# A four-layer attention and adapter kernel: the first tile's weight folding and tables in a new order, the narrow weight products with exchanged sides, and filled waits at the end

## The chip, the cores and the metric

The kernel runs on one core of a Trainium2 chip. It is one program with an instruction stream for each engine: TensorE (PE; its weight loads are shown as PEld), VectorE (DVE), ScalarE (ACT), GpSimd (POOL) and SyncE (SP), which only issues DMAs. The streams are written by hand and meet at semaphores. The metric is the device time of one execution in microseconds.

## The reference

The input x is 32 sequences of 64 tokens with 512 features, in float32. Four residual layers follow one another.

```
x = x + attention(x)          # 8 query heads, 4 key heads of 64; rms norm, rotation;
                              # the new keys and values go into a paged cache of 16-token
                              # blocks, and 256 positions of it are attended to
x = x + W1[subject] applied to each sequence           # 64 x 64 matrix per sequence
x = x + x@W_base.T + scale*(((x@Wt.T)@A[e].T)@B[e].T)@Wp.T   # e: adapter of the sequence
x = x + x@W.T + scale3*((x@A3[e3].T)@B3[e3].T)
```

## The kernel before

**Tiles.** The 2048 tokens are 16 tiles of 128 (two sequences each). A prologue makes the new keys and values of all tiles (`key_tile`, 16 of them), stores them to `newkv` in DRAM (`store_kv`, L364), and prepares the weights. Then one loop body is run per tile: attention of tile t, and, interleaved with it on every engine, the layers after attention of tile t-1. The last tile's rest has no attention beside it and stands alone at the end (`end = Tile(4, 0)`).

**Folding.** Layers 3 and 4 are both linear, so the kernel works with the product of their weights. `m23` is (W_base + I)(W + I), 512 x 512, made in four pieces by `fold(k)` (L1145, four matmuls each of 128 x 512 in float32); ScalarE and VectorE split each piece into a high and a low part (`m23_high` L677, `m23_low` L960). The identity is added to both weights by `add_identity` on GpSimd (L499) after their loads (SyncE, L394, from step `LATE_A` of the loop on). The adapters are folded as well: `down2` is Wt times A and `up2t` is Wp times B, each made by `narrow` (L1261: for each of four blocks of 128 rows four matmuls, the weight as the stationary side, 64 columns moving); `down3` is W_base's block times A3 (L1261, 128 columns moving), `cross` and `up2` are products of `up2t` with A3 and W (L1145), and four tables `up_s` are made by `carried(e)` on TensorE (L1299) and `carry(e)` on VectorE (L1116). SyncE stores the tables to DRAM, and for each tile the sequences' rows are picked from them.

**Names in the loop body on TensorE.** `queries` (L1152, L1157: query product of the next tile, in high and low parts), `queries_t` (L1204: its transposes), `keys_t` (L1308: transposes of gathered keys), `scores` (L1322), `probs_t` (L1335: transposes of probabilities), `values` (L1346: two heads in two halves of the array's columns), `project` (L1152, L1157), `layer1` (L1369), `ranks` (L1380), `layer3` (L1390), `layer3_low` (L1395), `layer3_ranks` (L1400). Scalar copies of `layer1`'s result are L744 and L739, the residual is L1049, the output copy is L754.

**GpSimd's order.** It computes inverse roots for the key tiles (`root`, L481), then adds the identities, then gathers cache rows (L512, L519) and the new keys (`lay_over`, L526) for the first attention batches, which waits for all stores of `newkv`.

**The eight PSUM banks** are `gb`, `sbk`, `tb`, `ob`, two of each. In the first tile `fold(2)` and `fold(3)` use `ob`, and `carried` uses `gb` and `ob`. Parts of the SBUF are used first for setup and later for the loop: the new order needs `wb_s`, `w3_s` and the tables for longer.

## Time and profile before

| | |
|---|---|
| median of 3 runs | 456.7 us (456.54 to 456.89) |
| profiled execution | 458.0 us, its span 456.2 us |
| mean granted TensorE clock | 0.985 of full |
| PE busy | 440.8 us (97%) |
| DVE, ACT, POOL busy | 308.8, 262.0, 228.5 us |
| DMA queues moved | 67.40 MB, mean 148 GB/s |

The span runs from the first to the last instruction; the execution's own time is 1.8 us longer. Three parts of the span matter below: the key tiles to about 63.5 us, the preparation and the first tile to about 129 us, and the end from about 441 us; between the last two lie fifteen loop bodies. In a list in order of time a line gives start, duration, engine, code line and operation, with the idle time before it and who ended it in brackets. The count of matmul rows is twice the number of float32 matmuls.

### The profile page before, as it was taken

What the parts mean: (1) busy time and instruction counts of PE and PEld (TensorE: products, weight loads), DVE (VectorE), ACT (ScalarE), POOL (GpSimd) and SP (SyncE); (2) the same over time, 40 slices, a digit from 0 to 9 for tenths busy, and PEclk for the clock granted to TensorE, in tenths of its full rate; (3) what the DMA queues carried; (4) which work ended last, traced back from release to release, by engine and by line L of the source; (5) the groups of instructions that cost most, each with busy time, mean ns of one, the idle gap of its engine ahead of it and who ended that gap; (6) DMA issues with size and microseconds to landing.
All of it is one profiled execution on the core that took longest, in us unless ns stands there. A gap on an engine that the chain in (4) does not pass through costs nothing.

```text
span 456.2 us, 10436 instructions
## 1 busy us (share of the span) xinstructions
PE 440.8 (97%) x3039; PEld 316.7 (69%) x3039; DVE 308.8 (68%) x899; ACT 262.0 (57%) x772; POOL 228.5 (50%) x245
## 2 busy tenths in 40 slices
PE   8999996999699999999999999999999999999996
PEld 3444884466377778777877777777777787777764
DVE  4688878655667677776767676767777676757531
ACT  0756850354357575756666475757575666656641
POOL 0225469665655657374655655564747465341000
PEclk9999997999899999999999999999999999999998
DMA  6577796264826465565647373746456563533131
GB/s 211 192 246 250 214 349 200 85 175 109 272 62 185 93 170 130 143 163 112 178 91 209 62 214 65 198 102 166 134 137 145 138 197 72 158 61 66 28 70 53
DMA packets 75593, 67.40 MB, mean 148 GB/s; under 512 B 50869, under 2 KB 51253, under 8 KB 75538
## 3 DMA queue, kind: packets, MB, share of 16 engines
q1 hardware_dynamic: 60208, 37.97, 30.9%
q0 software_dynamic: 14400, 28.05, 22.6%
q10 hardware_dynamic: 930, 0.72, 0.6%
q8 instruction: 25, 0.41, 0.4%
q14 instruction: 30, 0.25, 0.2%
HBM read 72.49 MB, written 10.22 MB: 181 GB/s over the span
## 4 chain that ended last, share of the span: by engine, by line
PE 90%; DVE 3%; issue 2%; POOL 2%; DMA 1%; ACT 1%; DVEq 0%; POOLq 0%; ACTq 0%
PE gb L1152 13%; PE sbk L1322 10%; PE ob L1346 10%; PE tb L1335 9%; PE gb L1181 7%; PE gb L1390 7%; PE gb L1157 6%; PE tb L1308 5%; PE gb L1395 4%; PE gb L1369 3%; PE gb L1400 3%; PE ob L1145 2%; PE ob L1380 2%; PE gb L1204 2%; PE sbk L1209 1%
## 5 line engine op out<-in xcount | busy, mean ns | idle before, releaser
L1031 DVE CUSTOM_DVE_ANT_0 wide<-sbk,mask 128x336 f32<-128x336 f32 x128 | 60.0, 505 | 63.4 <-PE sbk L1322 63.1
L728 ACT ACTIVATE pt_s<-tb 112x384 f32<-112x384 f32 x128 | 55.6, 488 | 53.5 <-PE tb L1335 53.5
L722 ACT ACTIVATE wide<-wide,negmax 128x336 f32<-128x336 f32 x128 | 72.6, 571 | 22.0 <-DVE negmax L1031 21.2
L526 POOL DMA_INDIRECT windows_more<-newkv,idx_b x48 | 49.0, 1021 | 61.9 <-issue 50.1
L526 POOL DMA_INDIRECT windows<-newkv,idx_b x48 | 49.8, 1038 | 47.7 <-issue 40.4
L1335 PEld LDWEIGHTS tb<-cst_late,wide 128*112 128x112 f32 x384 | 44.4, 133 | 18.9 <-issue 11.1
L1335 PE MATMUL tb<-cst_late,wide 128*112 128x128 f32 x384 | 52.5, 273 | 2.3 <-DVE wide L1044 1.5
L1322 PE MATMUL sbk<-kt_s,qt_s 64*128 64x336 f32 x256 | 52.8, 489 | 0.0
L1044 DVE TENSOR_SCALAR wide<-wide,rinv 128x336 f32<-128x336 f32 x128 | 45.4, 397 | 2.3
L716 ACT ACTIVATE kt_s<-tb 128x336 f32<-128x336 f32 x64 | 25.4, 449 | 13.3 <-PE tb L1308 13.2
L1181 PE MATMUL gb<-wkv_s,xt_s 128*128 128x512 f32 x72 | 31.9, 596 | 0.0
L481 POOL TENSOR_TENSOR k_rstd<-k_ms,half 128x4 f32<-128x4 f32 x16 | 18.9, 1181 | 23.1 <-DVE k_ms L892 23.0
L481 POOL TENSOR_TENSOR q_rstd<-q_ms,half 128x8 f32<-128x8 f32 x16 | 26.8, 1676 | 6.2 <-DVE q_ms L892 5.8
L890 DVE TENSOR_REDUCE q_ss<-q_sq 128x8 f32<-128x512 f32 x16 | 11.0, 686 | 25.8 <-ACT q_sq L652 25.8
L652 ACT ACTIVATE q_sq<-gb 128x512 f32<-128x512 f32 x15 | 9.0, 597 | 32.5 <-PE gb L1157 32.5
L1390 PE MATMUL gb<-m_hi,x_hi 128*128 128x512 f32 x64 | 27.3, 427 | 0.0
L1152 PE MATMUL gb<-wo_hi,ot_hi 128*128 128x512 f32 x64 | 26.5, 414 | 0.6 <-ACT ot_hi L734 0.6
L1390 PE MATMUL gb<-m_lo,x_hi 128*128 128x512 f32 x64 | 25.9, 404 | 0.0
L1346 PEld LDWEIGHTS ob<-pt_s,windows 112*64 112x64 f32 x384 | 20.6, 137 | 7.4 <-issue 3.7
L1346 PEld LDWEIGHTS ob<-pt_s,windows_more 112*64 112x64 f32 x384 | 20.6, 137 | 7.2 <-issue 3.9
L1322 PEld LDWEIGHTS sbk<-kt_s,qt_s 64*128 64x128 f32 x256 | 19.4, 185 | 8.9 <-issue 8.7
L1152 PE MATMUL gb<-wo_lo,ot_hi 128*128 128x512 f32 x64 | 25.2, 393 | 0.0
(217 smaller groups left out, 1026.8 us busy)
## 6 DMA issues: line engine op xcount, KB each, us to landing
xt_s<-xt_dram SPq DMA_DIRECT2D x31, 256.0 KB, 4.7
newkv<-kvo SPq DMA_DIRECT2D x16, 256.0 KB, 3.6
xtok_s<-xtok_dram SPq DMA_DIRECT2D x16, 256.0 KB
up_sel<-up_tab SPq DMA_DIRECT2D x128, 32.0 KB
out_dram<-xo SPq DMA_DIRECT2D x16, 256.0 KB, 4.1
down_sel<-down_tab SPq DMA_DIRECT2D x64, 32.0 KB
wkv_s<-wkv_dram SPq DMA_DIRECT2D x4, 256.0 KB, 6.1
wide<-wt_dram SPq DMA_DIRECT2D x4, 256.0 KB, 5.3
```

What stands on the lines that cost most here:

```text
L481: nc.gpsimd.tensor_tensor(nr[w]["rstd"][:], nr[w]["ms"][:], half[:, 0:h], ALU.pow).then_inc(S[w + "_rstd"], 1)
L526: nc.gpsimd.indirect_dma_start(kv_s[r][:, c, :], None, newkv, bass.IndirectOffsetOnAxis(ap=idx_b[r][:, (1, 2, 4)[c]:(1, 2, 4)[c] + 1], axi ...
L722: nc.scalar.activation(prob[i][:, g, :], neg_s[:, g, :], ACT.Exp, bias=negmax[:, g:g + 1], scale=-1.0, accum_out=psum_p[i][:, g:g + 1]).th ...
L728: nc.scalar.activation(pt_s[g][:], tb[g % 2][0:KP, 0:CH * 128].rearrange("p (c q) -> p c q", c=CH), ACT.Copy).then_inc(S["pt_ev"], 1)
L1031: V.tensor_tensor_reduce(out=neg_s[:, g, :], in0=sbk[g % 2][:, 0:WK], in1=mask[(t.part(u) + k) % 2][:], scale=-1.0 / 16, scalar=3.0e38, op ...
L1044: V.tensor_scalar(prob[i][:, g, :], prob[i][:, g, :], rinv[i][:, g:g + 1], None, ALU.mult).then_inc(S["prob_ready"], 1)
L1152: last = mm(bank, lhs(0, c), rhs(b, c), start=(c == 0 and b == 0), stop=False)
L1181: last = mm(gb[n % 2][:], xt_s[r][:, c, :], wkv_s[:, c, :], start=(c == 0), stop=(c == C - 1))
L1322: mm(sbk[h][:, 0:WK], qt_s[half_rows, 256 * p + 128 * v:256 * p + 128 * v + 128], kt_s[p][half_rows, :], start=True, stop=True).then_inc(S ...
L1335: last = nc.tensor.transpose(tb[g % 2][0:KP, 128 * c:128 * c + 128], prob[i][:, g, KP * c:KP * c + KP], ident)
L1346: last = mm(ob[u][64 * h:64 * h + 64, 128 * p:128 * p + 128], kv_s[r][:, c, 256 + 64 * g:320 + 64 * g], pt_s[g][:, c, :], start=(c == 0), ...
L1390: mm(gb[0][:], x2s[0][:, c, :], m23_s[b][:, c, :], start=(c == 0 and b == 0), stop=False)
```

## The change

It reorders preparation and the first loop body on every engine, and edits the end.

- `narrow` for `down2` and `up2t` is replaced: the 64-column adapter matrix is the stationary side, the weight's 512 columns move, `down2` in the lower 64 output rows and `up2t` in the upper 64 of one bank, alternately, eight matmuls in all. One copy (`both_s`), four transposes and two copies bring the result into the old layout.
- The identities are added by VectorE after key tiles 13 and 14; the weights' loads begin two steps earlier in SyncE's loop (`LATE_A` 8 for 10).
- In the first tile's body, `queries_t(2)` waits for three pieces' low parts (`m23_lo` 3) and the last `values` for four. ScalarE's `m23_high(2)` stands behind its `probs_t(0, 3)` there, `m23_high(3)` behind `probs_t(1, 1)`.
- `fold(0)` and `fold(1)` stay ahead of the first tile, `fold(2)` and `fold(3)` move into it; the four `carried` and `carry` move from the first tile to before it (`carry` on VectorE within its first norms), with other banks. `queries_t(1)` moves behind `down3` and `cross`, the first scores behind `up2`.
- On VectorE the first `query_tile` comes after the low parts; on GpSimd the first `lay_over` comes before the second gathers.
- At the end, one of the two copies of `layer1`'s result goes to VectorE, and two extra matmuls of 384 columns whose result nobody reads (`stay_awake`) stand behind `project` and behind `layer1`.
- The SBUF tensors of the loop are allocated in another order, with gaps; SyncE and ScalarE get waits that protect the shared regions.

```diff
@@ shared
-        LATE_A = TILES // 2 + 2
+        LATE_A = TILES // 2
@@ SyncE, tile
+                if first:
+                    sp.wait_ge(S["m23_mm"], C)
                 after(sp, S["x1_ready"], t.n(1, 0))
                 sp.dma_start(xtok_s[:], xtok[t.n(1, 0)]).then_inc(S["l_xtok"], 16)
@@ GpSimd
             root("k", 4, 16)
-            add_identity(wb_s, ("l_wb", 16 * C), "wb_ident")
-            add_identity(w3_s, ("l_w3", 16 * C), "w3_ident")
-            gather_pair(t0, 0, 1)
-            gather_single(t0, 0, 1)
...
             lay_over(t0, 0, 0)
+            gather_pair(t0, 0, 1)
+            gather_single(t0, 0, 1)
             root("q", 8, 1)
+            pool.wait_ge(S["l_scl"], 48)
+            pool.wait_ge(S["l_ab3"], 32)
+            P.tensor_scalar(b3_s[:], b3_s[:], scl3[:], 1.0, ALU.mult, ALU.mult).then_inc(S["b3_scaled"], 1)
             lay_over(t0, 0, 1)
-            pool.wait_ge(S["up2t_mm"], 1)
+            pool.wait_ge(S["both_mm"], 1)
@@ ScalarE, ahead of the loop
+            evac(both_s, ob[0][:], "both_mm", "both_ev")
+            both = ob[1][:].rearrange("p (c w r) -> p w c r", c=C, w=2)
+            evac(down2_s[:].rearrange("p e c r -> p c e r"), both[:, 0].rearrange("p c (e r) -> p c e r", e=NE2), "both_t_mm", "down2_ev")
+            evac(up2t_s[:], both[:, 1].unsqueeze(2).to_broadcast([128, C, 2, 64]), "both_t_mm", "up2t_ev")
             m23_high(0, tb[0])
             split_high(5)
-            square(1, sbk[0])
+            m23_high(1, tb[1])
             split_high(6)
             split_high(7)
-            m23_high(1, tb[1])
-            queries(1, 0, sbk[1])
-            m23_high(2, ob[0])
+            square(1, sbk[0])
             xq_high(2, xt_s[0], 32)
-            m23_high(3, ob[1])
@@ ScalarE, behind keys(Tile(0, 0), 0, 0)
-            exps(Tile(0, 0), 0, 0, 0)
-            exps(Tile(0, 0), 0, 0, 1)
             evac(down3_s[:].rearrange("p e c r -> p c e r"),
                  gb[0][:].rearrange("p (c e r) -> p c e r", c=C, e=NE3), "down3_mm", "down3_ev")
-            exps(Tile(0, 0), 0, 0, 2)
-            exps(Tile(0, 0), 0, 0, 3)
             evac(cross[:], ob[1][:, 0:64], "cross_mm", "cross_ev")
+            queries(1, 0, sbk[1])
+            act.wait_ge(S["up2_mm"], 1)
+            act.wait_ge(S["l_scl"], 48)
+            nc.scalar.activation(up2_s[:], gb[1][:], ACT.Copy, scale=scl2[:]).then_inc(S["up2_ev"], 1)
+            for g in range(G):
+                exps(Tile(0, 0), 0, 0, g)
@@ ScalarE, end
-            layer1(end)
+            act.wait_ge(S["l1_mm"], TILES)
+            nc.scalar.activation(x2t[:, :, 0:64], gb[1][:, 0:256].rearrange("p (c t) -> p c t", c=C), ACT.Copy).then_inc(S["x2_ready"], 1)
+            act.wait_ge(S["x2_half"], 1)
@@ VectorE
                 key_tile(n)
+                if n == 13:
+                    add_identity(wb_s, "l_wb", "wb_ident")
+                elif n == 14:
+                    add_identity(w3_s, "l_w3", "w3_ident")
...
+            m23_low(0, tb[0])
             split_low(4)
-            m23_low(0, tb[0])
-            dve.wait_ge(S["qtab_ready"], 1)
-            query_tile(Tile(0, 0), 0, None, None, None, sbk[0])
             split_low(5)
             m23_low(1, tb[1])
             split_low(6)
             split_low(7)
+            dve.wait_ge(S["qtab_ready"], 1)
+            query_tile(Tile(0, 0), 0, None, None, None, sbk[0])
@@ VectorE, tile
                 norm(t, 0, 0, (0, 1))
                 if first:
-                    dve.wait_ge(S["cross_ev"], 1)
-                    V.tensor_tensor(cross_s[:], cross[:].unsqueeze(1).to_broadcast([128, NE3, 64]),
-                                    con("hot3").unsqueeze(2).to_broadcast([128, NE3, 64]), ALU.mult).then_inc(S["cross_ready"], 1)
+                    for e in range(NE3 // 2):
+                        carry(e)
...
                 def between():
                     if first:
-                        carry(0)
-                        carry(1)
+                        m23_low(2, gb[1])
...
                 if first:
-                    carry(2)
-                    carry(3)
+                    m23_low(3, ob[1])
@@ VectorE, end
             attn_residual(end)
+            dve.wait_ge(S["l1_mm"], TILES)
+            V.tensor_copy(x2t[:, :, 64:128], ob[1][:, 0:256].rearrange("p (c t) -> p c t", c=C)).then_inc(S["x2_half"], 1)
@@ TensorE, ahead of the loop
-            narrow(ob[0], 64, lambda c, k: wt_s[:, c, 128 * k:128 * k + 128], lambda c: a2_s[:, c, :]).then_inc(S["down2_mm"], 1)
             pe.wait_ge(S["l_wpt"], 16 * (C + 1))
-            narrow(ob[1], 64, lambda c, k: wpt_s[:, c, 128 * k:128 * k + 128], lambda c: b2_s[:, c, :]).then_inc(S["up2t_mm"], 1)
+            for c in range(C):
+                mm(ob[0][0:64], a2_s[:, c, :], wt_s[:, c, :], start=(c == 0), stop=(c == C - 1))
+                last = mm(ob[0][64:128], b2_s[:, c, :], wpt_s[:, c, :], start=(c == 0), stop=(c == C - 1))
+            last.then_inc(S["both_mm"], 1)
             pe.wait_ge(S["wb_ident"], 1)
             pe.wait_ge(S["w3_ident"], 1)
             pe.wait_ge(S["idx_ready"], 1)
-            fold(0)
+            fold(0, tb[0])
+            pe.wait_ge(S["both_ev"], 1)
+            for c in range(C):
+                last = nc.tensor.transpose(ob[1][:, 128 * c:128 * c + 128], both_s[:, 128 * c:128 * c + 128], ident)
+            last.then_inc(S["both_t_mm"], 1)
+            fold(1, tb[1])
             pe.wait_ge(S["split_lo"], C)
             queries(1, sbk[0])
-            fold(1)
-            queries_t(1, sbk[1])
-            fold(2)
-            fold(3)
@@ TensorE, tile
                 probs_t(t, 0, 3, False)
-                if not first:
+                if first:
+                    pe.wait_ge(S["up_ev"], NE3 // 2)
+                    fold(2, gb[1])
+                else:
                     layer1(t)
...
-                if not first:
+                if first:
+                    fold(3, ob[1])
+                else:
                     layer3(t, not last)
@@ TensorE, behind keys_t(t0, 0, 0)
+            narrow(gb[0], 128, lambda c, k: wb_s[:, c, 128 * k:128 * k + 128], lambda c: a3_s[:, c, :]).then_inc(S["down3_mm"], 1)
+            pe.wait_ge(S["up2t_ev"], 1)
+            dense(ob[1][:, 0:64], lambda c: a3_s[:, c, :], lambda c: up2t_s[:, c, 0, :]).then_inc(S["cross_mm"], 1)
+            queries_t(1, sbk[1])
             pe.wait_ge(S["k_copied"], TILES)
             dense(gb[1][:], lambda c: up2t_s[:, c, :, :].rearrange("p a r -> p (a r)"),
                   lambda c: w3_s[:, c, :]).then_inc(S["up2_mm"], 1)
-            pe.wait_ge(S["m23_lo"], C)
-            dense(ob[1][:, 0:64], lambda c: a3_s[:, c, :], lambda c: up2t_s[:, c, 0, :]).then_inc(S["cross_mm"], 1)
+            for g in (0, 2):
+                scores(t0, 0, 0, (g, g + 1))
+            for e in range(NE3 // 2):
+                carried(e)
@@ TensorE, end
+            def stay_awake():
+                mm(sbk[0][:, 0:384], qrot[:, 0:128], qrot[:, 0:384], start=True, stop=True)
+
             project(end, False)
+            stay_awake()
             layer1(end)
+            stay_awake()
+            pe.wait_ge(S["x2_half"], 1)
             ranks(end)
```

## Rows read from the trace of the kernel before

**Rows 1.** Page, busy time and share of the span by engine.

```profile
PE 440.8 (97%) x3039; PEld 316.7 (69%) x3039; DVE 308.8 (68%) x899; ACT 262.0 (57%) x772; POOL 228.5 (50%) x245
```

**Rows 2.** Chain of waits, in order of time: start, us, work.

```profile
121.34 1.72 PE ob L1299 x2
...
150.41 1.86 PE gb L1152 x8
...
171.53 1.86 PE gb L1152 x8
```

**Rows 3.** TensorE in order of time, 63 to 125 us.

```profile
63.46 3.68 PE L1261 MATMUL ob<-a_s,wide 128*128 128x64 f32 x32
66.97 3.74 PE L1261 MATMUL ob<-windows,wide 128*128 128x64 f32 x32
74.21 5.91 PE L1145 MATMUL tb<-w_s,wb_s 128*128 128x512 f32 x8 [3.50 <-issue]
...
82.71 3.59 PE L1145 MATMUL tb<-w_s,wb_s 128*128 128x512 f32 x8
87.33 0.66 PE L1204 MATMUL sbk<-cst_late,qrot 128*128 128x128 f32 x4 [1.03 <-DVE qrot L914]
...
111.03 1.53 PE L1346 MATMUL ob<-pt_s,windows 112*64 112x128 f32 x24
...
119.09 0.63 PE L1204 MATMUL gb<-cst_late,qrot 128*128 128x128 f32 x4 [1.99 <-DVE qrot L914]
...
124.55 0.84 PE L1335 MATMUL tb<-cst_late,wide 128*112 128x128 f32 x6 [1.51 <-DVE wide L1044]
```

**Rows 4.** Stretches of 2 us: length, PE, PEld, DVE, ACT, POOL busy, granted clock, DMA.

```profile
70.00:72.00 2.00, 0.71 (x7) 0.57 (x6) 1.80 (x1) 0.60 (x1) 2.00 (x6) 0.98 0.71 256
...
78.00:80.00 2.00, 2.00 (x5) 0.77 (x5) 1.48 (x3) 0.00 (x0) 1.70 (x2) 0.82 0.95 292
...
118.00:120.00 2.00, 0.91 (x5) 0.70 (x6) 0.95 (x2) 0.62 (x2) 1.51 (x2) 0.92 0.99 197
```

**Rows 5.** GpSimd in order of time, 68 to 78 us.

```profile
68.91 1.26 POOL L481 TENSOR_TENSOR k_rstd<-k_ms,half 128x4 f32<-128x4 f32 x1
...
71.80 2.31 POOL L499 TENSOR_TENSOR w_s<-w_s,cst_late 128x128 f32<-128x128 f32 x4
...
77.63 1.50 POOL L526 DMA_INDIRECT windows<-newkv,idx_b  x1 [0.30 <-issue]
```

**Rows 6.** VectorE in order of time, 65 to 71 us, and at 441 us.

```profile
65.62 0.28 DVE L901 TENSOR_TENSOR k_t<-kvo,ksin 128x128 f32<-128x128 f32 x1
...
67.51 0.42 DVE L914 TENSOR_TENSOR kvo<-k_t,k_rstd 128x256 f32<-128x256 f32 x1 [0.94 <-POOL k_rstd L481]
...
70.20 2.74 DVE L914 TENSOR_TENSOR kvo<-k_t,k_rstd 128x256 f32<-128x256 f32 x1 [0.94 <-POOL k_rstd L481]
...
441.33 0.42 DVE L1057 TENSOR_TENSOR ot_lo<-ob,ot_hi 128x256 fp32r<-128x256 f32 x1 [3.83 <-ACT ot_hi L734]
```

**Rows 7.** SyncE's queue in order of time, one of the late loads.

```profile
55.45 0.45 SPq L394 DMA_DIRECT2D w_s<-w_dram  x1
```

**Rows 8.** DMA issues of 60 to 90 us: KB each, median us to landing.

```profile
newkv<-kvo SPq DMA_DIRECT2D x5, 256.0 KB, 3.7
...
windows<-newkv,idx_b POOLq DMA_INDIRECT x6, 3.0
```

**Rows 9.** Chain of waits at the end of the span.

```profile
444.48 0.70 DVE x L1049
...
446.38 0.67 ACT x2t L744 x2
...
447.09 0.89 PE ob L1380 x8
447.98 3.35 PE gb L1390 x8
```

**Rows 10.** A stretch of 1 us at the end, columns as in rows 4.

```profile
447.00:448.00 1.00, 0.91 (x9) 0.58 (x9) 0.27 (x1) 0.67 (x2) 0.00 (x0) 0.69 0.00 0
```

More of the change, by code:

```diff
@@ L287, in build @@
         mask = [sb(f"mask{i}", [128, WK]) for i in range(2)]
-        xtok_s = sb("xtok_s", [128, 512])
         down_sel = [sb(f"down_sel{i}", [128, C, 64]) for i in range(2)]
-        pt_s = [sb(f"pt_s{i}", [KP, CH, 128]) for i in range(G)]
-        up_sel = [sb(f"up_sel{i}", [128, 512]) for i in range(2)]
-        ot_s = [sb(f"ot_{w}", [128, 4, 128], f32r) for w in ("hi", "lo")]
         x1 = sb("x1", [128, 512])
@@ L297, in build @@
         xo = sb("xo", [128, 512])
+        up_sel = [sb(f"up_sel{i}", [128, 512]) for i in range(2)]
+        xtok_s = sb("xtok_s", [128, 512])
+        sb("rest_of_w3", [128, 64])
+        ot_s = [sb(f"ot_{w}", [128, 4, 128], f32r) for w in ("hi", "lo")]
+        sb("tables_below", [128, (NE2 + NE3) * C * RANK + C * 128 + 512 + 64 + NE3 * 64 + C * 64])
+        pt_s = [sb(f"pt_s{i}", [KP, CH, 128]) for i in range(G)]
         gb = [ctx.enter_context(nc.psum_tensor(f"gb{i}", [128, 512], f32)) for i in range(2)]
@@ L494, in _ @@
                             con("ident", NB)[:, 0:NB].unsqueeze(1).to_broadcast([NB, BLOCKS, NB]), ALU.mult).then_inc(S["blkd_ready"], 1)
-            def add_identity(w, loaded, done):
-                pool.wait_ge(S[loaded[0]], loaded[1])
-                for c in range(C):
-                    d = w[:, c, 128 * c:128 * c + 128]
-                    last = P.tensor_tensor(d, d, ident, ALU.add)
-                last.then_inc(S[done], 1)
             def copy_index(t, u, k):
@@ L782, in tile @@
                 probs_t(t, 1, 1)
+                if first:
+                    m23_high(3, ob[1])
                 if not last:
@@ L1417, in tile @@
                 values(t, 0, 1)
-                if first:
-                    carried(0)
-                    carried(1)
-                else:
+                if not first:
                     ranks(t)
@@ L1425, in tile @@
                     keys_t(t, 1, 1)
-                if not first:
+                if first:
+                    fold(3, ob[1])
+                else:
                     layer3(t, not last)
@@ L1433, in tile @@
                     else:
-                        pe.wait_ge(S["up_ev"], 1)
+                        pe.wait_ge(S["m23_lo"], 3)
                     queries_t(t.n(1, 2), gb[1])
-                if first:
-                    carried(2)
-                    carried(3)
-                else:
+                if not first:
                     layer3_low(t)
```

63 lines of the change are left out of this document (23 added, 40 removed).

## The prediction

> **What bounds the kernel now.** I read the page first: TensorE is busy 97% of the span, the next engine 68% [rows 1]. The chain of waits says the same of the repeated tiles: the query product starts at 150.41 and at 171.53, 21.1 us apart, with only TensorE work of other lines between [rows 2]. No edit touches the repeated work, so the fifteen bodies keep their time, and only what lies ahead of them and behind them can move. There I read TensorE in order of time and the granted clock beside it. Up to 63.5 us the key tiles run without a gap. Then the reader is to see four gaps, of 3.50, 1.03, 1.99 and 1.51 us [rows 3], and twice a fall of the granted clock to its lower level, 1.2 in place of 2.4 GHz: around 72 us, back by 79, and just before 120 us [rows 4]. Each fall follows a stretch in which TensorE did little: the first the narrow products and the start of the 3.50 us gap, the second the 1.99 us gap. A third fall is at the end [rows 10].
>
> **The early part, step by step.**
>
> *Narrow products.* Before: two groups, 3.68 and 3.74 us in the list; from 63.46 to the end at 70.71 they take 7.25 us [rows 3]. After: eight float32 matmuls of 512 columns. One such matmul is 3.59/4 = 0.90 us [rows 3], the fold at 82.71. They write two halves of the columns alternately, as `values` does: its 12 matmuls of 128 columns take 1.53 us [rows 3], 0.13 each, where a quarter of 0.90 would be 0.22 each. So halves overlap: four pairs, 4 x 0.90 = 3.6 us. Without overlap they would take 7.2 us, the other bound; I take the first, since the `values` row is the same alternation with different moving data. Four transposes are added, 0.66 us as L1204 shows [rows 3]. The copy of the bank lies beside `fold(0)`; without this cover it would cost some 0.6. Sum 4.3 for 7.25: **-3.0**.
>
> *The identities.* Before, GpSimd adds them behind its last root (68.91 + 1.26) and ends at 74.1 [rows 5], and the first fold starts at 74.21. After, VectorE does it in eight adds of 128 x 128; the nearest row, with two SBUF inputs and the same size, is 0.28 long and frees the engine after 0.21, L901 [rows 6]: 0.85 us a weight, at most 8 x 0.28 = 2.2 in all. The second weight's adds follow key tile 14, whose last step starts at 67.51 and takes 0.42 [rows 6], so they end at 68.8; the next root, which started at 68.91 [rows 5], gets its input just in time. Loads: the weights' last piece now stands two steps earlier, in the step whose row is 55.45 [rows 7]; with 3.7 us to landing of a piece of this size [rows 8] it is there well before 65. Four pieces, 1 MB, pass SyncE's queue ahead of x loads and stores that they stood behind; at the 292 GB/s of a full stretch [rows 4] that is 3.6 us at most, if every one of them were awaited. TensorE shows no gap up to 63.5 that such a load ended, and from the third of these steps on the queue holds what it held before, so I take nothing. TensorE is done with the products at 67.1, so the gap is 1.7 for 3.50: **-1.8** (bounds: gap 1.0 to 3.0).
>
> The Trainium skill speaks against this step: "SBUF — State Buffer", section "Who interferes with whom", has a VectorE instruction with two SBUF inputs and a GpSimd instruction that reads SBUF exclude each other for a whole instruction. The trace shows both behaviours: a VectorE multiply stretched to 2.74 us while GpSimd added the identities [rows 6], but L901 at 0.28 beside a gather issue. By the rule the adds could wait out a root; the sum above does not use it.
>
> *The clock at the first fold.* `fold(0)` takes 5.91 at the lower level and 3.59 at the higher [rows 3]. With a gap halved and denser work ahead of it, I expect it to keep the higher: **-2.3** (other bound: nothing).
>
> *From there to the first body.* The 1.03 us gap [rows 3] is a wait for the first queries' rotation; after, the transposes stand behind `down3` and `cross` (some 5 us of TensorE work) and the rotation is long done: -1.0. Against it two new waits. `keys_t(0)` now follows the first queries at about 79.5 (68.8, two folds, transposes, and 1.86 [rows 2] + 0.9 of queries). Its gather of new keys waits for the last store: rotation ends at 70.6 (the 2.74 us row becomes 0.43 as the additions beside it are gone), the store takes 2.0 to 3.7 [rows 8], three gathers of 1.3 each (a row of 0.99 to 1.50 and 0.30 before it [rows 5]) follow, the last landing 3.0 after its issue [rows 8]: 79 to 80.5. GpSimd began this at 77.63 before [rows 5]. I take +0.4. And the second pair of scores waits for the first pair's maxima with nothing between, where `down3` stood before: +0.6. The products `up2`, `cross`, `down3` and four `carried` only move. Net **0**. The first body then starts at about 95.5 for 106.0; 3.4 of this is work that only moves, two folds into the body for four `carried` out of it.
>
> *The first body.* Out go the gaps 1.99 and 1.51 [rows 3] and the low clock in the last two `carried`, the second of them 1.72 [rows 2], the other nearly as long, for 0.90 each: 1.5. In come the two folds. Their weights must stay, therefore SyncE loads `xtok` after `fold(3)`, at about 111; it is needed near 121. Behind `fold(3)` a new gap opens ahead of `probs_t(1, 2)`: ScalarE copies two probability tiles, then the high part, VectorE makes the low part and then the norm that is waited for, about 2.8 us in a row, of which `probs_t` and `queries_t` cover 1.1. The nearest row is the wait for the same norm in the same place, 1.51 [rows 3]. I take 1.7, bounds 0.5 and 2.5. 3.5 + 1.5 - 1.7: **-3.3**. What is queued behind on VectorE is `split_attn`, not needed before the next body. SyncE stores the up tables after `xtok`, some 5 us earlier than before, and they are first read in the second body.
>
> Early sum: -3.0 - 1.8 - 2.3 - 0 - 3.3 = **-10.4**.
>
> **The end.** The chain has two copies in a row on ScalarE, 0.67, then `ranks` 0.89 and `layer3` 3.35 [rows 9], the latter two at a clock that falls in the stretch of 447 [rows 10]; eight such matmuls take 1.86 at the higher [rows 2]. The fall follows the gaps around `layer1`: one while VectorE adds the residual, 0.70, and one under the copies, 0.67 [rows 9]. After: an extra matmul of 384 columns is 0.90 x 384/512 = 0.67 us. The first fits under the residual. The second starts at 446.36 and ends at 447.0. The two halves of x2t go beside each other, half of 0.67 on ScalarE and 0.42 on VectorE (nearest row of 256 columns from PSUM [rows 6]), ready at 446.85, so the second extra matmul costs `ranks` 0.15 against this, and `ranks` starts at 447.0 for 447.09. The high part is ready at 447.5 for 447.9: -0.4. Eight matmuls at the higher clock: 3.35 to 1.86, -1.5. Together **-2.0**; without the clock only -0.4. If the extra matmuls were not hidden they would cost 1.3.
>
> **Sum.** -12.4. The profiled execution took 458.0 with a span of 456.2, so its like would be 445.6; it was 1.3 over the median of the runs, 456.7, from which I count: 456.7 - 12.4 = **444.3 us**.
>
> **The rivals.**
>
> A. *The new gap behind `fold(3)` lowers the clock again.* The gap of 1.99 us did so, the one of 1.51 did not [rows 3, 4]; mine is 1.7. Such a fall cost 1.5 in `carried` and 2.3 in `fold(0)`. Time 444.3 + 1.7 = 446.0. Likewise a fall behind the 1.7 us gap ahead of `fold(0)`, 446.6.
>
> B. *The stores and gathers set the start.* If the last store lands late or GpSimd's list (some 27 gather issues of 1.3 us between 74 and 112) slips, `keys_t(0)`, the first root and the first body slip one to one: with a landing of twice the median [rows 8] about +3: 447.3. For: this wait is on the path by my own count. Against: the queue is emptier at 72 to 76 us than before.
>
> C. *The halves do not overlap at 512 columns.* +3.6 on the products, of which 1.7 fall into the gap: 446.2. Against: `values`.
>
> D. *The extra matmuls do not hold the clock.* +1.6: 445.9.
>
> E. *The shared port.* VectorE's adds wait for a GpSimd root (1.26 [rows 5]) and delay the fold by 1.0: 445.3. By the rule named above this is what would happen.
>
> F. *Slower: the new SBUF places hurt the repeated tiles.* `pt_s` and `ot_s`, written and read in every body, move. If that made each of 15 bodies longer by 0.85 us, 12.8 us, the gain would be gone and the time 457 to 458. It decides from 0.82 us a body. For it speaks nothing in the trace: no row ties a duration to an address, and ScalarE is idle before the copies it makes there.
>
> G. *The change does not act:* the preparation is bound by something I missed, such as loads, and only the end gains less than 0.9. It needs a wait of 10 us where I see none.
>
> **How the numbers follow.** The sum as it stands 0.42, A 0.22, B 0.12, C 0.07, D 0.08, E 0.05, F 0.02, G 0.02. Own range of the sum: gap before the fold +-0.8, gap in the body -1.2 to +0.8, waits +-0.5, so 442.5 to 446. Two of A to E together reach 448.4; the range is 442.5 to 448.4 and leaves out F, G and rarer pairs. Within 0.2% means within 0.9 us, about what runs of this kernel can tell from no change. All cases but F and G are faster: 0.96 faster, 0.02 same, 0.02 slower.
>
> **What the profile after would show.** The products 3.6 us long at 63.5; the first fold at about 68.8 in 3.6 us; no stretch at the lower clock between 66 and 95; the first body's `probs_t` at about 96 and the second body's `project` at 118.7 for 129.1, its period to the third still 21.1; at the end `layer3` 1.9 us long, starting 0.4 us closer to `project`. Wrong would be: a wait of TensorE over 3 us anywhere between 67 and 119, products over 5 us, a granted clock under 0.9 in the last ten microseconds, or a body period over 21.3.

## The result

The changed kernel takes 450.97 us, the median of four runs (450.43 to 452.9), where the kernel before took 456.62 beside it. The ratio is 0.9871, its 95% interval 0.9841 to 0.99. That is faster by 5.7 us; the prediction had said 12.4 us and a time of 444.3 with a range from 442.5 to 448.4. Two more measurements of the same kernel on other chips gave 0.9885 and 0.9888. The profiled execution took 450.86 us with a span of 449.1; the page says of it, as [rows 1] did before:

```profile
PE 434.0 (97%) x2999; PEld 310.9 (69%) x2999; DVE 307.4 (68%) x908; ACT 262.2 (58%) x772; POOL 226.4 (50%) x237
```

TensorE in order of time, the stretch of [rows 3]:

```profile
66.84 0.59 PE L1281 MATMUL ob<-wide,a_s 128*64 128x512 f32 x1
66.84 0.59 PE L1282 MATMUL ob<-wide,windows 128*64 128x512 f32 x1
69.39 3.67 PE L1156 MATMUL tb<-w_s,wb_s 128*128 128x512 f32 x8 [1.96 <-issue]
72.90 0.60 PE L1290 MATMUL ob<-cst_late,xt_s 128*128 128x128 f32 x4
73.34 3.60 PE L1156 MATMUL tb<-w_s,wb_s 128*128 128x512 f32 x8
...
78.62 1.07 PE L1168 MATMUL sbk<-wq_hi,xq_lo 128*128 128x512 f32 x4
83.65 0.77 PE L1310 MATMUL tb<-cst_late,windows 112*128 112x112 f32 x6 [3.96 <-DMA windows<-newkv,idx_b]
84.25 5.38 PE L1272 MATMUL gb<-a_s,wb_s 128*128 128x128 f32 x32
...
101.58 0.88 PE L1337 MATMUL tb<-cst_late,wide 128*112 128x128 f32 x6 [0.25 <-ACT kt_s L710]
...
119.68 0.84 PE L1337 MATMUL tb<-cst_late,wide 128*112 128x128 f32 x6 [2.11 <-DVE wide L1052]
```

The products start at 63.78 and are done by 67.4, and `fold(0)` (69.39) runs at full clock, all nearly as forecast. The first queries end at 79.7, where 79.5 was forecast. Then TensorE stands still for 3.96 us ahead of `keys_t(0)`, until the gathered new keys have landed, where the prediction had 0.4. `down3` behind it (84.25) takes 5.38 us instead of 3.75, because the clock has fallen. Stretches of the same execution (length, busy times, granted clock, DMA share, GB/s):

```profile
78.00:84.00 6.00, 2.04 (x12) 1.44 (x11) 5.23 (x11) 1.73 (x4) 4.96 (x4) 1.00 0.24 46
84.00:88.00 4.00, 4.00 (x25) 4.00 (x24) 1.97 (x7) 0.79 (x2) 3.19 (x4) 0.58 0.46 155
```

TensorE is busy 2.04 of 6 us ahead of the fall, and the DMA engines have 46 GB/s to do: nothing heavy is in the way. The chain of waits tells what TensorE waits for:

```profile
69.48 1.54 POOL k_rstd L487
71.02 0.02 issue
71.05 0.44 DVE kvo L914
71.48 0.02 issue
71.50 2.00 DMA newkv<-kvo
...
73.78 0.51 issue
...
74.52 0.34 POOL windows L525
...
79.86 3.66 DMA windows<-newkv,idx_b
83.52 0.14 issue
83.65 0.77 PE tb L1310 x6
```

The last root ends at 71.02, the last keys are rotated, stored, in DRAM at 73.50. GpSimd has stood idle since its root, and another 1.02 us pass before its first gather starts at 74.52; the chain shows them as work of its sequencer and issue. Then it gathers, in order of time:

```profile
74.52 3.30 POOL L525 DMA_INDIRECT windows<-newkv,idx_b  x1 [3.51 <-issue]
78.13 1.43 POOL L525 DMA_INDIRECT windows<-newkv,idx_b  x1 [0.31 <-issue]
79.86 1.49 POOL L525 DMA_INDIRECT windows<-newkv,idx_b  x1 [0.30 <-issue]
```

The first of the three takes 3.30 us, where no gather in [rows 5] took more than 1.50. Of the 10.4 us forecast for the early part 4.9 are left: by the chain of waits the second body's `project` starts at 124.2 (129.1 before, 118.7 forecast). The repeated bodies are 21.1 us apart in both traces; all fifteen together are 0.7 us shorter, which was not looked into. The end is shorter by 1.5 us from `project` to the output copy. In the chain of waits, answering to [rows 9]:

```profile
440.74 0.84 PE sbk L1483 x2
441.58 0.59 PE ob L1382 x8
442.17 2.04 PE gb L1392 x8
```

### The profile page after: what moved, and what is told of

The parts are those of the page before. It is cut to its first block, busy times and chain, and to the rows that moved or that the text cites. A ratio compares the mean times of both kernels' runs of the same rounds, so it can differ in the third digit from the quotient of the medians.

```text
span 449.1 us, 10359 instructions
## 1 busy us (share of the span) xinstructions
PE 434.0 (97%) x2999; PEld 310.9 (69%) x2999; DVE 307.4 (68%) x908; ACT 262.2 (58%) x772; POOL 226.4 (50%) x237
## 4 chain that ended last, share of the span: by engine, by line
PE 89%; DMA 3%; POOL 3%; issue 2%; DVE 2%; ACT 1%; POOLq 0%; DVEq 0%; ACTq 0%
PE gb L1163 13%; PE sbk L1324 11%; PE ob L1348 10%; PE tb L1337 9%; PE gb L1192 7%; PE gb L1392 7%; PE gb L1168 6%; PE tb L1310 5%; PE gb L1397 4%; PE gb L1371 4%; PE gb L1402 3%; DMA newkv<-kvo 2%; PE ob L1382 2%; PE gb L1156 2%; PE gb L1215 1%
## 5 line engine op out<-in xcount | busy, mean ns | idle before, releaser
L525 POOL DMA_INDIRECT windows<-newkv,idx_b x48 | 52.2, 1087 | 52.7 <-issue 42.8
```

Source lines behind the costliest of these rows:

```text
L525: nc.gpsimd.indirect_dma_start(kv_s[r][:, c, :], None, newkv, bass.IndirectOffsetOnAxis(ap=idx_b[r][:, (1, 2, 4)[c]:(1, 2, 4)[c] + 1], axi ...
```

## The experiments

Kernels that are compared with each other ran on one chip, and the chips differ: the kernel before took 457.4 to 457.9 us on three of them (e5 to e8, e13 to e16, e17) and 461.7 to 462.8 on three others (e1 to e4, e9 to e12, e18). On the latter ScalarE waits 2 to 7 us in the first body for something the profile does not name, in versions of the kernel before too (e3, e4, e10). So a whole time is compared only through the ratio to before on its own chip.

**The wait ahead of `keys_t(0)`: take it away, or shorten what it waits for.** e1 puts `keys_t(0)` of the first tile behind `down3`, `cross` and `queries_t(1)`; ScalarE's copies follow.

```diff
-            pe.wait_ge(S["m23_lo"], 2)
-            keys_t(t0, 0, 0)
             # down3, cross
             queries_t(1, sbk[1])
+            pe.wait_ge(S["m23_lo"], 2)
+            keys_t(t0, 0, 0)
```

> The changed kernel with the first key transposes moved behind down3, cross and the query transposes (ScalarE's copy of them likewise). Theory: the 3.96 us wait for the gather of new keys, and the stretch at the lower clock behind it (1.5 us in down3), are the missing time; with 5 us of ready TensorE work ahead of the transposes both go, so 445.0 to 446.0 us, no gap over 0.5 us at that place, granted clock full from 84 to 89 us. Rival: the first body is bound by the gathers and roots behind the first one (GpSimd's list); then the gap only moves to the scores or the second transposes and the time stays at 449 to 451.

e2 gathers the second block's old keys ahead of GpSimd's wait for the stores.

```diff
+            gather_pair(t0, 0, 1)
+            gather_single(t0, 0, 1)
             for i in range(4):
                 pool.wait_ge(kv_stored[i], 16 * TILES // 4)
             lay_over(t0, 0, 0)
-            gather_pair(t0, 0, 1)
-            gather_single(t0, 0, 1)
```

> The changed kernel with GpSimd's gathers of the second batch's cache rows put back ahead of the wait for the last store, where GpSimd sits idle for 3.5 us. Theory: the first gather of new keys is released by the store and not by these, so the gap ahead of the first key transposes stays 3.5 to 4.5 us and the time within 1 us of 451. Rival: the 3.30 us that the first gather of new keys takes to issue is the price of being first after an idle stretch of GpSimd; then with other gathers ahead it falls to 1.5, the gap to about 2, the time to 448 or 449.

e1: 0.9871 (0.9834 to 0.9909). The gap is gone and `down3` has the full clock, but `fold(0)` ran at the lower one, and the first body holds the unnamed wait, 4.9 us on ScalarE; the ratio is that of the changed kernel elsewhere, which did not itself run on this chip. e2: 0.988 (0.9839 to 0.992), in time the same; but its rival was right about the gather. GpSimd in order of time in e2:

```profile
70.87 1.20 POOL L511 DMA_INDIRECT windows<-kvrows_dram,idx_b  x1 [0.19 <-issue]
72.38 1.43 POOL L518 DMA_INDIRECT windows<-kvrows_dram,idx_b  x1 [0.30 <-issue]
74.20 1.42 POOL L525 DMA_INDIRECT windows<-newkv,idx_b  x1 [0.39 <-issue]
```

The gather of new keys starts 0.3 us earlier than in the changed kernel and takes 1.42. So 3.30 is no property of that gather.

e8 does both edits at once, beside e5, the changed kernel unaltered.

> The changed kernel unaltered, as the control of this call. Expected: about 0.987 of the kernel before, a gap of about 4.0 us on TensorE ahead of the first tile's first keys_t, the first of the three gathers of new keys taking 3.3 us on GpSimd and the other two about 1.5 each, and the down3 product at the lower clock (about 5.3 us).

> The changed kernel with both moves at once: keys_t(0) of the first tile behind down3, the cross products and the query transposes on TensorE and ScalarE, and the second block's old pairs and single gathered ahead of the wait for the stored new keys on GpSimd. If the gap ahead of keys_t(0) with the clock that falls behind it is the missing gain, and nothing behind it waits again: no gap over 0.7 us between the fold of the first half and the first scores, down3 at 3.75 us, first body begun 4 to 5 us earlier than in the unaltered changed kernel, and the whole 3 to 5 us (0.7 to 1.1 per cent) faster than it. Rival: the first body then waits at another place for ScalarE and VectorE, as it did in the run with TensorE's order alone changed, and the whole is within 1 us of the changed kernel.

e5: 452.08 us, 0.9885 (0.9854 to 0.9916). e8: 448.64 us, 0.9805 (0.9773 to 0.9836), 3.4 us faster than e5. TensorE in e8:

```profile
79.84 3.73 PE L1272 MATMUL gb<-a_s,wb_s 128*128 128x128 f32 x32
83.41 1.00 PE L1156 MATMUL ob<-up2t_s,a_s 128*128 128x64 f32 x8
85.54 0.66 PE L1215 MATMUL sbk<-cst_late,qrot 128*128 128x128 f32 x4 [1.13 <-DVE qrot L914]
```

No gap between the queries and `down3`, which keeps its clock. The theory holds: the wait of `keys_t(0)` was where a good half of the missing gain went, 3.4 of 6.7 us, with 2 us of uncertainty by the two ratios. Next in line stands the queries' rotation, 1.13 us, above the 0.7 that was expected: with two gathers sent ahead, ScalarE waits 2.77 us for the load of a piece of `wo`; that this is what delays VectorE's mean squares was read from the trace and not tested. e5 shows something else: there `fold(0)` ran at the lower clock (5.37 us), and the gap ahead of `keys_t(0)` was only 1.73, with `keys_t(0)` at 83.30 and `down3` at 3.75. Whatever TensorE loses or wins ahead of the gather's landing does not move `keys_t(0)`. Yet e5 is not ahead of the changed kernel's first profile by the 1.6 us that `down3` saves: its second body's `project` starts at 123.8 for 124.2. Behind `fold(3)` the clock falls in e5:

```profile
117.68 1.34 PE L1337 MATMUL tb<-cst_late,wide 128*112 128x128 f32 x6 [2.11 <-DVE wide L1052]
118.95 1.49 PE L1324 MATMUL sbk<-kt_s,qt_s 64*128 64x336 f32 x4
```

With the `values` behind them (1.96) these take 0.84, 0.84 and 1.53 us in the first profile, after the same gap of 2.11 us. The granted clock of 118 to 120 and 120 to 122 us is 0.50 and 0.68 in e5, 1.00 in both in the first profile. It falls in this place in e7 and e15 too, and costs 1.6 us each time.

**What makes the gather long.** Three diagnoses on the changed kernel: VectorE idle while the gathers are issued (e6), the table stores held back (e7), the angle tables and the `wq_lo` subtractions exchanged on VectorE (e9).

```diff
+            dve.wait_ge(kv_new[0], 16 * CH)        # e6, ahead of the query angle tables
+            sp.wait_ge(S["q_rot"], 1)              # e7, ahead of the store of w1_tab
-            for i in range(C):                     # e9: these two behind the tables
-                split_low(i)
             for n in range(4):
                 last = angle_table(V, "q", n)
             last.then_inc(S["qtab_ready"], 1)
+            for i in range(C):
+                split_low(i)
```

> The changed kernel with one wait added: VectorE starts the query angle tables only once the first block's new keys have been gathered, so that it is idle while GpSimd issues these gathers. Theory V (VectorE's work beside GpSimd makes the first gather long): the first gather of new keys falls from 3.3 us to about 1.5. Rival W (the gather is long for what lies ahead of it on GpSimd's own queue or in the transfers): it stays at about 3.3. Either way the queries start late, and the whole is 2 to 6 us slower than the changed kernel; only the gathers' lengths are read.

> The changed kernel with the stores of the picked layers' and the down tables held back until the first query tile's rotation has been made, so that no store of a table is in flight while the new keys are gathered. Theory T (transfers of the tables in the queues lengthen the first gather): it falls from 3.3 us towards 1.5, and the gap ahead of keys_t from 4.0 to about 2.2. Rival W (it is what the gather waits for on GpSimd itself, its own index or code, whatever SyncE moves): it stays at 3.2 to 3.4 and the gap at 4.0.

> The changed kernel with one reordering on VectorE: the four products of the query angle tables (2.4 us) ahead of the four wq_lo subtractions (2.4 us) and no longer behind them, so that the subtractions, and not the tables, lie beside the first gather of new keys. Theory P (it is the tables' products, or how many microseconds of VectorE's work happen to lie there, that stretch this gather): the first gather falls from 3.3 us to 1.0 to 1.5, the keys land some 2 us earlier, the gap ahead of keys_t(0) falls from 4.0 us to about 2 (or from 1.7 to nothing where the fold ran at the lower clock), and the whole is 1 to 2 us faster than the unaltered changed kernel. Rival Q (any work of VectorE stretches the first gather behind an idle GpSimd): it stays at 3.3 us and nothing changes.

GpSimd in e6, then in e7:

```profile
75.55 1.06 POOL L525 DMA_INDIRECT windows<-newkv,idx_b  x1 [3.51 <-issue]
```

```profile
75.63 3.30 POOL L526 DMA_INDIRECT windows<-newkv,idx_b  x1 [3.51 <-issue]
```

e6 bears out theory V (454.38 us in its one run, slower for the wait that was put in), e7 refutes theory T (451.51), and e9 (0.9859, 0.982 to 0.9898, on a chip with the unnamed waits) shows 3.29 us: it does not matter which of VectorE's work lies there. But VectorE is as busy in e2 and e8, where the gather takes 1.4. What differs there is GpSimd: it had issued two gathers shortly before and had not stood idle. e17 puts arithmetic there instead, an instruction that the kernel has anyway.

```diff
             for i in range(4):
                 pool.wait_ge(kv_stored[i], 16 * TILES // 4)
+            pool.wait_ge(S["l_scl"], 48)
+            pool.wait_ge(S["l_ab3"], 32)
+            P.tensor_scalar(b3_s[:], b3_s[:], scl3[:], 1.0, ALU.mult, ALU.mult).then_inc(S["b3_scaled"], 1)
             lay_over(t0, 0, 0)
```

(the three lines stood behind the queries' root).

> The changed kernel with the scaling of the up3 weights (one GpSimd instruction of 0.7 to 1.2 us) moved from behind the queries' root to between the wait for the stored new keys and the first gather of them. Theory I (GpSimd had been idle, and the first instruction behind the wait pays): the scaling itself takes the extra time or the gather falls to about 1.5 us, its end moves by less than 0.5 us against the unaltered changed kernel. Rival J (it is the first gather since the queue stood still, whatever arithmetic goes ahead): the gather still takes 3.3 us, the keys land 0.9 us later, and the whole is 0.5 to 1.5 us slower than the changed kernel.

```profile
73.63 1.72 POOL L585 TENSOR_SCALAR b_s<-b_s,scl 128x512 f32<-128x512 f32 x1 [2.83 <-DMA newkv<-kvo]
75.53 1.34 POOL L525 DMA_INDIRECT windows<-newkv,idx_b  x1 [0.18 <-issue]
```

The scaling takes 1.72 us in the place of 0.7 to 1.2, the gather 1.34, and the first gather ends at 76.87, 0.95 earlier than in the changed kernel although more is done ahead of it. The scaling starts 0.35 us behind the landing of the keys (73.28), and the sequencer's work for the gather, the 1.02 us of the changed kernel, now lies under it. So the 0.95 us are both: the wait for the start hidden, and the gather shorter. Theory I holds as against rival J, with more gain than it gave. That the idle time is the cause is still an inference: the scaling is long too, and beside it a product of VectorE is, two of them taking 1.69 us for 1.29. The whole: 449.88 us, 0.9822 (0.9796 to 0.9848), from moving three lines; the changed kernel had 0.9871 to 0.9888 on its chips. TensorE still waits 0.82 us for the landing, at 82.02.

e18 takes e17 and moves `keys_t(0)` as e1 does.

> The version with the scaling of the up3 weights ahead of the first gather of new keys, and in addition keys_t(0) behind down3, the cross products and the query transposes on TensorE and ScalarE. If keys_t(0) was the last wait of that stretch: down3 begins right behind the queries, the wait ahead of the query transposes is under 0.5 us (1.1 with two gathers ahead, which held the queries' weights up), and the whole is 0.979 to 0.981 of before. Rival: the queries' rotation takes its place, and the whole stays at 0.982.

It gave 0.9838 (0.9792 to 0.9883), above both forecasts; the interval reaches down to them. In the preparation it does what was said: `down3` starts at 80.98, and the list shows no gap ahead of it or of the query transposes. But this chip has the unnamed wait, at its longest here:

```profile
114.68 0.38 ACT L728 ACTIVATE ot_hi<-ob 128x256 fp32r<-128x256 f32 x1 [6.68 <-remote]
```

e12 is e8 with one more move on ScalarE in the first body.

```diff
+                if first:
+                    m23_high(3, ob[1])
                 probs_t(t, 1, 0)
                 probs_t(t, 1, 1)
-                if first:
-                    m23_high(3, ob[1])
```

> The version with the keys behind down3 and the old gathers first, and in addition ScalarE makes the high part of the third fold ahead of the two copies of the probabilities in the first body, to shorten the wait of TensorE for the normalised probabilities there (2.1 us in the changed kernel, 1.5 and 0.5 in the version without this edit). If that wait hangs on ScalarE's order: it falls by about 0.5 us, and the whole is 448 us where the version without it gave 448.6 beside 457.6 for before (0.979 of before). Rival: GpSimd's late root of the queries sets the place, and nothing changes (0.980 to 0.981).

It gave 0.9789 (0.9751 to 0.9826), not to be told from e8; the gap in question went from 0.47 to nothing, but `queries_t` ahead of it waits 1.42 us for the low part, where it waited 1.50 for the rotation in e8.

**The parts one by one.** e3 is the kernel before with the exchanged products alone, e4 with the end's edit alone, e10 and e13 with the identities and their loads alone, e14 with identities and products, e15 is everything, e16 everything with the loads at their old steps, e11 everything without the two extra matmuls. The edits of e3, e4, e10, e13 and e14 are the parts of the change's own diff that bear these names, put into the kernel before; in e3 and e14 its first tile keeps its order.

```diff
-        LATE_A = TILES // 2            # e16, in the changed kernel
+        LATE_A = TILES // 2 + 2
-            stay_awake()               # e11, both
```

> The kernel before with the exchanged products alone (one bank, copy, four transposes). Theory: products end near 67.0 in place of 70.7, but the first fold waits for GpSimd's identities until 74.2 anyway, so the gain goes into the wait (7.1 us in place of 3.5) and the transposes add 0.5: 456.6 to 457.6 us, no gain. Rival: the products are worth their 3 us by themselves, 453.5.

> The kernel before with the edit of the end alone (two extra matmuls, the copies of x2t on two engines). Theory: as in the changed trace, 1.5 us less from the last project to the end of the span, and the clock stays full: 455.0 to 455.3 us. Rival: the extra matmuls do nothing for the clock and the gain is only the parallel copies, 0.2 to 0.4 us, 456.3.

> The kernel before with the identities' part alone: the additions on VectorE inside the key phase and the late weight loads moved two tiles earlier. By the terms of the prediction: the gap of 3.5 us ahead of fold(0) and its lower clock (2.3) go, GpSimd's gathers start 1.5 to 2 us earlier, and the moved loads cost 0.3 to 0.8, so 3 to 5 us (0.7 to 1.1 per cent) faster than before. Rival: the new keys' gather now sets the start of keys_t(0), a gap of about 3 us stands there and the gain is under 2 us.

> The kernel before with the identities' part alone (additions on VectorE, late loads two tiles earlier), again, as the base of this call. Expected: 0.988 of before, as in its first run: some 5.5 us.

> The same with the exchanged products and their transposes in addition, the old order of the first tile and the old end. In this order the folds stand ahead of the first keys_t, and a wait for the queries' rotation stands behind them. Theory (the products' 3.0 us are real, and go where TensorE then waits for something that TensorE doesn't set: the adds and the evacuation ahead of fold(0), then the queries' weights, split from loads): 0 to 1.5 us faster than with the identities alone, with gaps ahead of fold(0) and ahead of the query transposes that are 2 to 3 us longer together. Rival (nothing takes it back in this order, only the changed kernel's own order does): 2.5 to 3 us faster than with the identities alone.

> The changed kernel unaltered, for this call's sum: 0.987 to 0.9885 of before. Beside the identities alone that leaves, after the 1.9 us of the end, minus 1 to minus 2 us for the products and the new order together.

| run | what | ratio to before | interval |
|---|---|---|---|
| e3 | products alone | 1.0031 | 1.0001 to 1.0061 |
| e4 | end alone | 0.9958 | 0.993 to 0.9985 |
| e10 | identities alone | 0.9879 | 0.9844 to 0.9914 |
| e13 | the same, on e14's chip | 0.9905 | 0.9881 to 0.993 |
| e14 | identities and products | 0.9886 | 0.9864 to 0.9908 |
| e15 | everything | 0.9888 | 0.9862 to 0.9914 |

The products gain nothing alone: with the identities still on GpSimd, the gap ahead of `fold(0)` grows from 3.50 to 7.02 us. TensorE in e3:

```profile
74.26 5.82 PE L1146 MATMUL tb<-w_s,wb_s 128*128 128x512 f32 x8 [7.02 <-issue]
```

On top of the identities they bring 1.1 us (452.05 against 453.19), which the intervals do not tell from nothing. TensorE in e13, then in e14:

```profile
67.46 3.74 PE L1263 MATMUL ob<-windows,wide 128*128 128x64 f32 x32
71.04 3.65 PE L1147 MATMUL tb<-w_s,wb_s 128*128 128x512 f32 x8
...
82.49 0.66 PE L1206 MATMUL sbk<-cst_late,qrot 128*128 128x128 f32 x4 [1.23 <-DVE qrot L905]
```

```profile
69.89 3.67 PE L1148 MATMUL tb<-w_s,wb_s 128*128 128x512 f32 x8 [1.98 <-issue]
73.40 0.60 PE L1287 MATMUL ob<-cst_late,xt_s 128*128 128x128 f32 x4
75.03 0.51 PE L1155 MATMUL sbk<-wq_hi,xq_hi 128*128 128x512 f32 x1 [1.03 <-DVE wq_lo L925]
...
83.19 0.66 PE L1207 MATMUL sbk<-cst_late,qrot 128*128 128x128 f32 x4 [1.67 <-DVE qrot L906]
```

In e13 the long products cover VectorE's work and there is no gap ahead of `fold(0)`. Shorten them, and two gaps open, 1.98 and 1.03 us, and a third grows by 0.44. The query transposes start no earlier than without the products' edit.

The end's row needs a caution. With the old end `layer3` ran at the lower clock in the kernel before (3.35) and in e10 (3.50), but at the full one in e3 (2.11), e13 and e14. The chain of waits of e13:

```profile
444.55 0.66 PE ob L1382 x8
...
445.21 2.12 PE gb L1392 x8
```

From `project` to the output copy the old end takes 10.23 us in e3, e13 and e14, the new one 10.17. So where the clock does not fall, the end's edit is worth 0.06 us, and nearly all of the trace's 1.5 us is whether it fell in that execution.

Identities, products and the end add up to about 0.9886 - 0.0042 = 0.9844; everything together gave 0.9888. So the new order of the first tile costs 2.0 us by these ratios instead of bringing 3.3; each of the three is uncertain by 1 us and more either way, so that it brings nothing is as far as the figure carries.

> The changed kernel with the late weight loads two tiles later, as in the kernel before. The prediction costed their move at nothing. If their traffic is what holds TensorE before the last key tiles (a wait of ScalarE for new keys in the way to be stored, 2.1 us against 1.7 before): the last key tiles start 0.3 to 0.8 us earlier. Against it, the weights for the additions then arrive later, VectorE waits for them inside the key phase, and the last keys are rotated and stored later: the new keys' gather and with it the first keys_t move by 2 us or more, and the whole is 1 to 4 us slower than the changed kernel.

e16: 0.9889 (0.9866 to 0.9911), the same as e15 on its chip. It shows the slack most plainly. VectorE waits 2.38 us for the weights, `fold(0)` starts at 70.67 at the lower clock and takes 6.51 us, the queries end at 83.8, and yet:

```profile
70.67 6.51 PE L1156 MATMUL tb<-w_s,wb_s 128*128 128x512 f32 x8 [3.88 <-issue]
...
84.05 0.76 PE L1310 MATMUL tb<-cst_late,windows 112*128 112x112 f32 x6 [0.23 <-DMA windows<-newkv,idx_b]
```

`keys_t(0)` starts at 84.05, and at 83.86 in e15 on the same chip, 83.65 in the changed kernel's first profile, where the queries were over by 79.7. What is lost ahead of it, 4.1 us against that profile, costs nothing, because it was slack. The first side of its expectation came on TensorE: the loads' move does hold up the last key tiles, with a gap of 0.97 us among them in e15 and none in e16. The loss of the other side did not: `keys_t(0)` moved by 0.2 us and the whole not at all.

> The changed kernel without the two extra matmuls of 384 columns in the last tile. By the prediction they hold TensorE's clock through the end: without them layer3 runs at the lower clock (2.9 to 3.4 us and not 2.0) and the whole is about 1 us (0.2 per cent) slower than the changed kernel. Rival: the waits are short enough with the two column halves alone, layer3 stays near 2.0 us, and the whole is the same or 0.1 us faster.

e11: 0.9896 (0.9854 to 0.9938). Its chain of waits at the end:

```profile
442.92 0.43 DVE x2t L1144
443.36 0.05 issue
443.40 0.66 PE ob L1382 x8
444.06 0.01 issue
444.08 2.11 PE gb L1392 x8
```

`layer3` keeps the full clock without the extra matmuls, and from `project` to the output copy it is 10.02 us against 10.17 with them. So they cost 0.15 us where the clock holds anyway. Whether they keep it from falling is open: it is full in every trace with them, but full too in e11 and in three of the five with the old end.

## Why the prediction was wrong

Sign and the larger part of the mechanisms were right, the size was not: 5.7 for 12.4 us. The step that failed is the one that let the new keys' gather cost 0.4 us.

**Products, -3.0.** Right as to TensorE: 63.78 to 67.4, the halves overlap, C falls. Wrong as a gain: of the 3.0 us 1.1 arrives at most (e14 against e13), because VectorE's chains to `fold(0)` and to the queries end later than the shortened work.

**Identities -1.8, clock -2.3.** Right in sum where they stand alone: e10 and e13 measure 5.6 and 4.3 us for 4.1; there no gap is left ahead of `fold(0)`, and it has the full clock. In the changed kernel the gap is 1.96 for 1.7, and the clock's 2.3 us were luck: of its three profiled executions one has `fold(0)` at the full clock, e5 and e15 at the lower. The loads' move, put at nothing, held the last key tiles up by 0.3 us in the first profile (products at 63.78 for 63.46). E did not happen: four adds take 0.89 us, as counted. But they lay beside gathers and not beside a root, so the case it feared was not met.

**From there to the first body, net 0 with +0.4 for the new keys' gather: this is the step that failed.** The wait is 3.96 us. Three terms of that estimate are too small and one is missing. The rotation ends at 71.5 for 70.6: the key tiles come 0.3 us later, and the last two roots take 1.48 and 1.54 for 1.20 and 1.26. The second weight's adds stand ahead of the last root's input (69.39), but GpSimd is itself busy with a gather until 69.42, so they are not shown to cost anything. From the landing of the keys to the first gather's start 1.02 us pass, which the sum did not have. The first two gathers, each counted as 1.3 with its pause, take 3.30 and 1.43 and two pauses of 0.3. The last lands 3.66 us after its issue, for 3.0. Only the store's 2.00 was at the good end. Together 83.5 for 79 to 80.5. Beneath the sizes lies an error of kind: the sum took every microsecond won on TensorE ahead of that point as won in the end, and left only 0.4 for the chain behind the stores, though both numbers, 79.5 and 80.5, stood a microsecond apart. In this order, once the two chains are level, nothing won on TensorE ahead of `keys_t(0)` counts. That start, 83.3 to 83.9 us in all three profiles of the changed kernel for 79.9 forecast, is the steady part of the miss; the length of the wait ahead of it is not (3.96, 1.73, 1.77), since it depends on when TensorE arrives.

**The clock.** In the first profile it fell behind the 3.96 us, which is neither in the sum nor among A's two places, and cost `down3` 5.38 - 3.75 = 1.6 us. A itself did not come in that execution: the gap behind `fold(3)` is 2.11 (forecast 1.7, bounds to 2.5) at a clock of 1.00. In the other two profiles of the same kernel it was the other way round: `down3` had the full clock, and A came at both its places. Ahead of `fold(0)`, 5.37 for 3.67 us, it cost nothing, since `keys_t(0)` was waiting anyway; behind `fold(3)` it cost 1.6 us, close to its price of 1.7.

**First body, -3.3.** The wait of the second pair of scores is 0.84 for 0.6 and the new gap 2.11 for 1.7. The sum of all misses up to the second body in the first profile: 3.6 for the wait, 1.6 clock, 0.2, 0.4, which is 5.8; 5.5 is what lies between the 118.7 us forecast and the 124.2 measured (123.8 in e5, 124.4 in e15).

**The end, -2.0.** Right in size, by luck: e4 gave 1.9 us (0.7 to 3.2 by its interval), the trace 1.5. The copies beside each other were to bring 0.4 and bring 0.06 with the extra matmuls, 0.2 without (10.23 against 10.17 and 10.02). The rest is the clock, and that fell with the old end in only two of five traces, so 1.5 us for it was counted as if it fell always. D did not happen; that the extra matmuls are what prevents it is not shown.

B was the rival that happened, at 0.12, and even its 3 us were too few. In two of three profiles A came with it. By the prediction's own prices the two together make 444.3 + 1.7 + 3 = 449.0, outside the range, which took its two-rival bound at 448.4. F falls: 21.1 us a body in both.

## What to carry to other kernels

Where the start of a transpose or a matmul is set by a chain of root, store, gather and landing, work out the end of that chain before counting anything ahead of it; when the two are within a microsecond, count the TensorE gains as zero and look for what shortens the chain. Here a single GpSimd instruction, moved to right behind a wait and ahead of the gather (e17), gained 2 to 3 us on top of the change by the ratios of different chips, and moving a waiting transpose behind other work together with earlier gathers (e8) gained 3.4. An edit that gains nothing alone (e3) or on top of another (e14) has to be priced together with what covers it. And a fall of the clock seen in one trace is not yet a cost that an edit removes: look for it in a second execution first. At the end of this kernel it was missing in three of five.

## What the runs showed of the hardware

**A gather's issue depends on what VectorE does and on what GpSimd did just before.** Issued by GpSimd behind an idle wait of 3.5 us, with VectorE at work on float32 operands in SBUF, the first gather takes 3.29 to 3.31 us, in all eight traces that have this order (the changed kernel's, e1, e5, e7, e9, e11, e15 and e16). With VectorE idle it takes 1.06 (e6). With VectorE at work, but other GpSimd instructions shortly ahead, it takes 1.34 to 1.50 (e2, e8, e10, e12 to e14, e17, e18, and the kernel before). By the Trainium skill, "SBUF — State Buffer", "Who interferes with whom", VectorE's two-input additions and products are held (inferred there) not to be in the way of a gather's descriptors. The measurements differ, at least in this place: 3.30 for 1.06. Whether it is the idle time on GpSimd that makes it worse, and why, was not settled.

**The clock is a matter of single executions.** With the same gap of 1.94 to 1.97 us ahead of it, `fold(0)` ran at the full clock in the changed kernel's profile and in e8, and at the lower in e5, e15 and e17. Behind the same gap of 2.11 us the first body kept it in the changed kernel's profile and lost it in e5, e7 and e15. With the same old end `layer3` took 3.35 and 3.50 us before and in e10, and 2.11 to 2.12 in e3, e13 and e14.

**The three chips on which the kernel before took 461.7 us and more show a wait in the first body that the profile calls remote,** 2.3 to 6.7 us on ScalarE; it is there in the kernel before with one edit (3.34 in e3, 3.20 in e4). It is longest in e18 (6.68), e1 and e12 (4.9), which order the first tile otherwise, but e10 and e11 come to it about as early as e1 and wait 3.3. So that it hides part of an early gain on those chips is possible and not shown. Its cause stayed open.
